# The order of work on five engines from one planned run, and six PSUM banks in one pool, in a macaron block (FFN, attention, FFN)

## The reference, cut to what matters

```python
def moe(x):                                       # 8 experts, D = F = 256
    weights = golden_weights(x, Wr, temperature)  # sigmoid, zone, top 2 as fallback, normalised
    gate = einsum('btd,edf->betf', x, Wg); up = einsum('btd,edf->betf', x, Wu)
    e_out = einsum('betf,efd->betd', silu(gate) * up, Wd)
    return einsum('bte,betd->btd', weights, e_out)
x = x + 0.5 * moe(layernorm(x))
x = x + attention(layernorm(x))                   # 16 heads of 16, causal, biases on q, k, v, out
x = x + 0.5 * moe(layernorm(x))
```

## Time and profile before

| | |
|---|---|
| median of 3 runs | 823.6 us (821.93 to 824.05) |
| profiled execution, its own time | 822.55 us |
| its span, first to last instruction | 820.8 us |
| PE busy | 767.7 us, 94% |
| DVE busy | 477.1 us, 58% |
| GpSimd (POOL) busy | 417.6 us, 51% |
| ACT busy | 342.1 us, 42% |
| mean granted TensorE clock | 0.991 |
| DMA | 81.56 MB, mean 99 GB/s |

### The profile page before, as it was taken

How to read it: one execution, slowest core, us unless ns; L and a number is a source line. 1 busy time by engine, 2 the same in 40 slices (tenths; PEclk the granted TensorE clock), 3 DMA queues, 4 the chain that set the end, 5 groups by cost and what they waited for, 6 DMA issues and landing times.

```text
span 820.8 us, 13838 instructions
## 1 busy us (share of the span) xinstructions
PE 767.7 (94%) x4878; PEld 608.1 (74%) x4878; DVE 477.1 (58%) x1314; ACT 342.1 (42%) x657; POOL 417.6 (51%) x499
## 2 busy tenths in 40 slices
PE   6787998989999999998999998899999999999998
PEld 6566877957768767676777766667777777888887
DVE  5657774485657654669654575955556732455333
ACT  4243434515347344264543454444435443332222
POOL 3465555535555453463544554445355555556663
PEclk9799999999999999999999999999999999999999
DMA  5524432533333413122431331245313212223332
GB/s 174 188 83 154 135 109 71 158 84 106 100 86 98 136 59 105 51 93 91 125 119 40 110 85 59 78 136 137 83 43 113 78 48 98 78 78 107 110 98 70
DMA packets 60805, 81.56 MB, mean 99 GB/s; under 512 B 8384, under 2 KB 44608, under 8 KB 60736
## 3 DMA queue, kind: packets, MB, share of 16 engines
q1 hardware_dynamic: 58544, 80.36, 31.8%
q10 hardware_dynamic: 2192, 0.32, 0.2%
HBM read 67.78 MB, written 12.71 MB: 98 GB/s over the span
## 4 chain that ended last, share of the span: by engine, by line
PE 71%; DVE 12%; issue 4%; POOL 4%; ACT 3%; DMA 1%; SPq 1%; POOLq 0%; ACTq 0%; DVEq 0%
PE gu L478 12%; PE gu L479 11%; PE gu L480 11%; PE dn L500 6%; PE dn L501 6%; PE dn L502 6%; PE ra L611 4%; PE ra L584 4%; PE ra L599 4%; DVE junk L997 2%; PE ra L455 2%; DVE hid L941 1%; DVE hid L949 1%; DVE stats L915 1%; POOL hid L1085 1%
## 5 line engine op out<-in xcount | busy, mean ns | idle before, releaser
L1085 POOL TENSOR_TENSOR hid<-hid,wb 128x512 f32<-128x512 f32 x124 | 160.6, 1295 | 182.5 <-DVE hid L949 182.1
L478 PE MATMUL gu<-xt_hi,wgu_hi 128*128 128x512 f32 x512 | 230.5, 450 | 13.4 <-DVE hid L941 8.2
L1089 POOL TENSOR_TENSOR ht_lo<-hid,ht_hi 128x512 fp32r<-128x512 f32 x124 | 160.5, 1294 | 142.7 <-ACT ht_hi L728 142.6
L479 PE MATMUL gu<-xt_hi,wgu_lo 128*128 128x512 f32 x512 | 204.3, 399 | 0.0
L997 DVE CUSTOM_DVE_ANT_0 junk<-ra,mask 128x128 bf16<-128x128 f32 (+3 forms) x256 | 124.0, 488 | 136.9 <-PE ra L584 134.7
L480 PE MATMUL gu<-xt_lo,wgu_hi 128*128 128x512 f32 x512 | 203.4, 397 | 0.0
L500 PE MATMUL dn<-wd,ht_hi 128*128 128x256 f32 x512 | 163.3, 319 | 2.9 <-POOL ht_lo L1089 2.9
L941 DVE SCALAR_TENSOR_TENSOR hid<-hid,gu 128x512 f32<-128x512 f32 x125 | 85.6, 685 | 126.4 <-ACT hid L720 125.7
L778 ACT ACTIVATE probs<-ra 128x512 f32<-128x512 f32 x160 | 94.9, 595 | 130.8 <-PE ra L599 130.2
L728 ACT ACTIVATE ht_hi<-hid 128x512 fp32r<-128x512 f32 x124 | 77.9, 628 | 161.0 <-POOL hid L1085 141.4
L501 PE MATMUL dn<-wd,ht_hi 128*128 128x256 f32 x512 | 144.2, 282 | 0.0
(11 more groups left out here) (165 smaller groups left out, 867.3 us busy)
## 6 DMA issues: line engine op xcount, KB each, us to landing
wd<-wd_parts SPq DMA_DIRECT2D x56, 512.0 KB, 3.5
wb<-wts_rows SPq DMA_DIRECT2D x62, 256.0 KB, 3.7
qk_parts<-parts SPq DMA_DIRECT2D x32, 192.0 KB, 2.1
q_st<-qk_parts SPq DMA_DIRECT2D x96, 64.0 KB, 3.2
k_st<-qk_parts SPq DMA_DIRECT2D x96, 64.0 KB, 2.4
wd_parts<-wd SPq DMA_DIRECT2D x8, 512.0 KB, 4.3
x_res<-in_x SPq DMA_DIRECT2D x4, 512.0 KB, 6.5
stage<-in_Wg SPq DMA_DIRECT2D x8, 256.0 KB, 4.5
```

What stands on the lines that cost most here:

```text
L478: mm(b_, w_hi, xt_hi[q % 2][:, c, :], start=c == 0, stop=False)
L479: mm(b_, w_lo, xt_hi[q % 2][:, c, :], start=False, stop=False)
L1085: nc.gpsimd.tensor_tensor(tb, tb, wb[m % NWB][:, :], ALU.mult).then_inc(hw_done, 1)
L1089: nc.gpsimd.tensor_tensor(ht_lo[n % NHT][:, :], hidden(n)[:, :], f32(ht_hi[n % NHT][:, :]), ALU.subtract).then_inc(lo_done, 1)
```

## The change

`spaced`, `DELAY` and `order_of` go. `schedule()` stays, and its times become targets. A new function `plan()` lists every item with its engine, an assumed length, and the items it needs; `Plan.run` goes once through the program in assumed time: whichever engine can start something earliest takes, of the items that could start within 0.1 us of its earliest, the one with the lowest rank (target plus a constant of the kind and engine). So an engine is given another item where the targeted one would still wait. It also keeps a common port of DVE and GpSimd that one of them holds at a time, the two `xn` buffers, and the banks: the item takes the bank that was freed first. The order of each engine and the bank of each use (`BANK`, `TURN`) go into the program. `g`, `u` and the former `ra` items share six banks; at most three of them for `g`/`u`, at most four for the rest. The number of PSUM banks is the same, eight with the two `dn`.

```diff
-NG, NA = 2, 4
+NBANK, NA, NG = 6, 4, 3
-BY_POOL = {"sg": (1, 2), "sd": (0, 1)}
+BY_POOL = {"sg": (1, 2), "sd": ()}
...
+FIRST = {"dve": {"t": -1.0, "h": -1.0, "max": 0.0, "sg": 0.0, "sd": 0.0, "stats": -0.2, "route": -0.5},
+         "act": {"t": -1.0, "hi": -0.8, "exp": 0.0, "sg": 0.0, "sd": 0.0},
+         "pool": {"exp": -0.3, "newton": -0.6, "xb": 0.0},
+         "pe": {}, "sp": {}}
+BEFORE = {"dve": -0.6, "act": -0.5, "pool": -0.5, "pe": 0.0, "sp": 0.0}
+AFTER_END = {"pe": 0.25, "act": 0.15, "dve": 0.12, "pool": 0.12, "sp": 0.0}
...
+                times = [(earliest(k), k) for k in open_[e]]
+                times = [x for x in times if x[0] is not None]
+                if not times:
+                    continue
+                t0 = min(times)[0]
+                t, key = min((x for x in times if x[0] <= t0 + 0.1), key=lambda x: (self.ops[x[1]]["rank"], x[1]))
+                if best is None or t < best[0]:
+                    best = (t, key)
...
+                b = min((x, i) for i, x in enumerate(bank_free) if x is not None)[1]
...
+            add(mine, ("ln", q, m), 0.75 if mine == "dve" else 1.0, ("pool" if k else "dve", "newton", k, 1), holds=("xn", m),
+                then=[routed(q - 1)] if q else [])
+            add("pe", ("xt", q, m), 0.45, (mine, "ln", q, m), last_of[q - 2] if q > 1 else None, lets=("xn", m))
...
+            add("act", ("aln", b, m), 1.0, ("pool", "newton", k, 1), holds=("xn", m))
...
+    add("act", ("bias",), 0.7, ("pool", "lo", NHID - 1))
+    add("dve", ("bias",), 1.0, ("act", "bias"), ("pe", "bias"))
+    add("pe", ("bias",), 0.71, ("act", "bias"), ("dve", "sa", 1), more=0.8)
...
         def rbank(it):
-            return ra[USE[it] % NA]
+            return ra[BANK[it]]
         def emptied(it):
-            return ra_free[USE[it] % NA], USE[it] // NA + 1
+            return ra_free[BANK[it]], TURN[it] + 1
...
-                        if USE[it] >= NA:
-                            pe.wait_ge(ra_free[USE[it] % NA], USE[it] // NA)
+                        if TURN[it] > 0:
+                            pe.wait_ge(ra_free[BANK[it]], TURN[it])
...
-                            if k >= NG:
-                                pe.wait_ge(gu_free, k - NG + 1)
+                            if TURN[use] > 0:
+                                pe.wait_ge(ra_free[BANK[use]], TURN[use])
```

More of the change, by code:

```diff
@@ L201, in schedule @@
     assert len({it for _, it in at}) == len(at)
-    return spaced({it: t for t, it in at})
-def spaced(t):
-    follower = {"qk": "ql", "mt": "mx"}
-    moved = True
-    while moved:
-        moved = False
-        uses = sorted((it for it in t if it[0] in RING), key=lambda it: t[it])
-        for before, it in zip(uses, uses[NA:]):
-            left = t[before] + DELAY[LAST[before[0]]][before[0]] + 0.01
-            if t[it] < left:
-                if it[0] in follower:
-                    t[(follower[it[0]],) + it[1:]] += left - t[it]
-                t[it] = left
-                moved = True
-                break
-    return [(x, it) for it, x in t.items()]
@@ L224 @@
-DELAY = {
[4 rows of a table removed]
-    "pool": {"exp": 0.2},
-    "sp": {"wt": 0.2, "ql": 0.4, "add": 0.3},
-}
-def order_of(at, engine):
-    late = DELAY.get(engine, {})
-    return [it for _, it in sorted(((t + late.get(it[0], 0.0), it) for t, it in at), key=lambda x: x[0])]
-LAST = {k: "act" for k in ("wbp", "wt", "v", "exp", "pv")} | {
-    k: "dve" for k in ("bias", "xt", "x", "z", "qk", "max", "mt", "t1", "t2", "wo")}
-RING = ("bias", "xt", "z", "wbp", "wt", "x", "qk", "v", "max", "mt", "exp", "pv", "t1", "t2", "wo")
+    return {it: t for t, it in at}
@@ new lines @@
+RING = ("bias", "xt", "z", "wbp", "wt", "x", "qk", "v", "max", "mt", "exp", "pv", "t1", "t2", "wo")
+FREED_BY = {k: "act" for k in ("wbp", "wt", "v", "exp", "pv")} | {
+    k: "dve" for k in ("bias", "xt", "x", "z", "qk", "max", "mt", "t1", "t2", "wo")}
+FIRST = {"dve": {"t": -1.0, "h": -1.0, "max": 0.0, "sg": 0.0, "sd": 0.0, "stats": -0.2, "route": -0.5},
+         "act": {"t": -1.0, "hi": -0.8, "exp": 0.0, "sg": 0.0, "sd": 0.0},
+         "pool": {"exp": -0.3, "newton": -0.6, "xb": 0.0},
+         "pe": {}, "sp": {}}
@@ L256, in dram @@
             return nc.dram_tensor(name, shape, dt, kind="Internal").ap()
-        at = schedule()
-        PE_ORDER, ACT_ORDER, DVE_ORDER, POOL_ORDER, SP_ORDER = (
-            order_of(at, e) for e in ("pe", "act", "dve", "pool", "sp"))
+        order, BANK, TURN = plan()
+        PE_ORDER, ACT_ORDER, DVE_ORDER, POOL_ORDER, SP_ORDER = (order[e] for e in ("pe", "act", "dve", "pool", "sp"))
         USE = {it: k for k, it in enumerate(it for it in PE_ORDER if it[0] in RING)}
+        MAX_USE = {it: k for k, it in enumerate(it for it in DVE_ORDER if it[0] == "max")}
+        MAX_AT = list(MAX_USE)
         ends = [it[1] for it in POOL_ORDER if it[0] == "newton" and it[2] == 1 and it[1] > 0]
@@ L267, in build @@
         for it in ACT_ORDER:
-            if it[0] in ("ln", "aln"):
+            if it[0] in ("ln", "aln") and it != ("ln", 0, 1):
                 if it[2] in latest:
                     XN_BEFORE[it] = latest[it[2]]
+                elif it[2] == 1:
+                    XN_BEFORE[it] = ("xt", 0, 1)
                 latest[it[2]] = ("xt" if it[0] == "ln" else "x",) + it[1:]
@@ L347, in build @@
         minus = over("minus", [96, 2 * NST * GH * T // 96], BF16, x2_at)
-        gu = [bank(f"gu{i}") for i in range(NG)]
         dn = [bank(f"dn{i}") for i in range(2)]
-        ra = [bank(f"ra{i}") for i in range(NA)]
+        ra = [bank(f"ra{i}") for i in range(NBANK)]
         wts_dram = dram("wts_rows", (NBLOCK, E, QT, P), F32)
@@ L397, in build @@
         ra_full = sem("ra_full")
-        ra_free = [sem(f"ra_free{i}") for i in range(NA)]
+        ra_free = [sem(f"ra_free{i}") for i in range(NBANK)]
         st_done = sem("st_done")
@@ L1079, in _ @@
                         tb = hidden(n)[:, :]
-                        pool.wait_ge(gu_free, 2 * n + 2)
+                        pool.wait_ge(*emptied(("u", n)))
                         if m < NWB:
```

282 lines of the change are left out of this document (269 added, 13 removed), and 4 rows, old and new, of the table DELAY.

## The result

The changed kernel takes **779.97 us** (median of 4 runs, 779.27 to 781.66), against 823.58 (821.93 to 824.05) before: the ratio is 0.9477, with a 95% interval of 0.9457 to 0.9497. It is 43.6 us faster. The forecast was 801, from 786 to 816: the direction is right, the size is half.

A forecast was written before the change was run, and what follows sets the result against it. TensorE, busy 94% of the span, was taken to bound the kernel through its waits and lower clock. -9 - 4 - 4.5 - 6 - 0.5 + 2 = -22 us from 822.55, with 1.05 to the median, gave 801, range 786 to 816.

The forecast's parts named there:

- The start's chain: First eight chunks: routing weights, then GpSimd's products and `newton`, set when `d` of chunk 3 starts; -9 us (-5 to -12).
- Chunk 8 "by 55": Sign at the end of the first eight chunks: chunk 8 begun by 55 us; after 59 the forecast is wrong.
- No wait of 3 us: Sign in the first 16 chunks: TensorE has no wait of 3 us or more before chunk 16.
- The wait before `bias`: Sign in block 1: TensorE still waits about 2 us before `bias`, for a small DVE product.
- Blocks 2 to 4: Chunks 32 to 80: waits for a bank named by turn go with the longest-free bank; -6 us of 16.7 (-12 to +6).
- the second eight chunks: Chunks 8 to 16: silu and product of chunk 9 move ahead of a weight subtraction; -4 us (0 to -6).
- block 1: Chunks 16 to 32: the wait of `x` for ACT's normalise goes, that before `bias` stays; -4.5 us (0 to -8).
- "+2": Whole kernel: 2 us added for waits that a plan of fixed lengths does not see.
- the start's clock: Sign in the first 60 us: TensorE's clock at 0.96 or more.
- More goes: Rival: every term comes out near its good end, -38 us in sum, 785 us; chance 0.08.
- The squeeze: Rival: attention of sequences 0 and 1 starts four chunks late with less filler, 832.5 us; chance 0.10.
- the last rival: The pool gives the same banks in turn, so only the orders count: 801 + 3 us; no chance of its own.

The follow-up runs named there:

- banks_only: The changed kernel with all five engines back in the hand-made order of before, the pool of six banks kept: 810.43 us.
- orders_only: The changed kernel with the old banks, two in turn for `g`/`u` and four in turn for the rest, orders planned for these: 783.86 us.
- free_act: The changed kernel's pool, ACT's order planned, the other four engines in the hand-made order, attention's `aln` ahead of the next `ln`: 796.89 us.
- act_by_hand: The changed kernel with ACT in the hand-made order of before, the other four engines and the banks planned: 784.93 us.
- bias_early: The changed kernel with DVE's small product for `bias` made an item of its own, placed early, which TensorE's `bias` needs in the plan: 775.17 us.

## Why the prediction was half right

**Right.** The kernel is bound by TensorE standing still, and the orders remove it. The start's chain came out close: weights 29.9 forecast, 29.80 measured; GpSimd's first product 32.0 and 32.01; its `lo` for chunk 3 done at 50.0, the forecast's "49.9 at most", with `newton` stretched again. The first of these is part luck: the prediction charged 2.1 us for the silus in front and gave no credit for the 3.1 us of stretching that went, but the routing's first maximum also started 3.0 us later (20.53 instead of 17.50), behind silu and product of chunk 0. The two cancel. Chunk 8 "by 55" was missed: it began at 55.94, for 7.6 us where 9 were forecast. No wait of 3 us is left after the first input. The wait before `bias` stayed, 1.60 us. No exponent waits for `x_lo` or a residual add.

**Wrong: the step "Blocks 2 to 4".** It gave "-6 us of 16.7", with a best case of -12; measured are -19.6. It priced only the waits that end with a bank in use. That part was sized well: with the pool alone (banks_only) chunks 32 to 80 take 343.0 us, 7.6 less. It named "the orders of DVE and ACT" among what can change there, and put them at nothing, without a reason. That is the step that failed: orders_only takes 331.9 there with the old banks, so the orders alone give 18.7. In the part where TensorE's order hardly differs, ACT's order alone takes 6.4 us more off than the pool (free_act), though it isn't the only one that can (act_by_hand). Of the 19.6 us, 15.7 are idle time and 3.9 are busy time (333.88 to 329.97). The best case, -12, stayed under the idle time; the stretch with its waits gone gave a little more than all of it.

**Too small: the second eight chunks and block 1.** "-4" and "-4.5" came out at 7.1 and 7.3. I priced the two or three waits over 2 us. Of the second eight chunks' 5.0 us idle and 1 to 2 of clock, all came back: with no idle time the clock is 1.00 instead of 0.96, an estimated 1.8 of the 7.1 (44.3 x 0.04). In block 1 idle time fell by 7.0, not only at the wait for `x`.

**The new waits.** "+2" for waits that a plan of fixed lengths can't see: the two for routing weights (1.6 us) and the one of a score for a silu (0.4) are such waits, 2.0 together. The measured gains by stretch have them inside already. Against these gains the terms are 1.4 too much at the start, and 3.1, 2.8, 13.6 and 1.3 too little in the others; with the "+2" on top, the miss is 21.4.

**Wrong: the start's clock.** 0.96 or more was forecast for the first 60 us, measured is 0.94. Of this, 1.5 us are what bias_early then wins back (it has 0.97 in its first 56); without them chunk 8 would begin at 54.4, inside the 53.5 to 54.5 of the forecast.

**The rivals.** "More goes" (785, chance 0.08) was the true case, and still 5 us short. It was held unlikely because three terms had to be at their good ends at once. I now read them as having one cause, a queue that has something ready at nearly every point, so that they go together. The squeeze did not come: from chunk 24 to chunk 49 (134.1 to 304.1) TensorE is idle 1.2 us, where more than 15 would have shown it, although the first `max` does come at chunk 28. Its "for it" rested on a wrong reading: 250.9 us of the earlier trace rows is the busy time of the weight loads, DVE's is 220.4, which is 0.63 of the stretch and not 0.72. And the pool isn't where the change lives: with it undone, 39.3 of 43.6 us remain; the 3 us that the last rival gave it measured 3.9.

## What to carry to other kernels

In an in-order queue on the engine that bounds the kernel, look first for short helper items that stand before their input is ready: each holds all the ready work behind it; moving a few of them by a chunk or so won 16 us here, and 9.6 us more of waits then stood at consumers that had not moved with them. In the first 16 chunks, banks alone moved such waits more than they removed them. When a change gives the queue something ready at every point, price it from the whole idle time of each stretch, with the named waits as the low end, and treat the terms as one chance, not as independent ones. Undo parts both ways, one alone and all but one: ACT's order was worth 13.5 us by the one and 5 by the other.
